# Self attention of a decoder layer: units per head, masks added in the pass for the maximum, outputs turned by the product, weights of q and k streamed

## What is computed

```python
h = x * rsqrt(mean(x * x) + EPS) * norm_w
q, k, v = (proj(w) for w in (w_q, w_k, w_v))        # 16 heads of 64
ll = einsum('bhnqd,bhnkd->bhnqk', qw, kw) * scale   # windows of 512: one per batch
ll = where(causal, ll, NEG)
scores = (einsum('bsd,do->bso', h, scorer_w) + scorer_b)[..., 0]
_, idx = top_k(scores, 128)                         # 128 tokens of the 512, by score
lg = where(idx <= pos, einsum('bhsd,bhgd->bhsg', q, kg) * scale, NEG)
attn = softmax(concatenate([ll, lg]))               # chosen tokens stand twice
o = attn[local] @ v + attn[chosen] @ vg
return x + o @ w_out
```

## Time and profile before

| what | value |
| --- | --- |
| median of 3 runs | 2310.07 us (2309.79 to 2315.15) |
| profiled execution | 2321.41 us, its span 2319.7 us |
| TensorE busy | 2134.8 us, 92% |
| VectorE busy | 1345.7 us, 58% |
| ScalarE busy | 844.9 us, 36% |
| GpSimd busy | 431.3 us, 19% |
| self attention | about 0 to 1556 us, eight batches, 184 us each |
| cross attention | about 1560 to 2080 us |
| routed block | the rest |

### The profile page before, as it was taken

The page is one execution under the profiler, slowest core; times in us unless marked ns, Lnnn a source line. Parts: engine busy times, 40 slices in busy tenths (PEclk is TensorE's granted clock), DMA queues, the critical chain, the costliest instruction groups (busy, mean ns, idle before and its releaser), DMA issues. The chain is left out here.

```text
span 2319.7 us, 35694 instructions
## 1 busy us (share of the span) xinstructions
PE 2134.8 (92%) x12029; PEld 1665.7 (72%) x12029; DVE 1345.7 (58%) x3145; ACT 844.9 (36%) x1541; POOL 431.3 (19%) x669
## 2 busy tenths in 40 slices
PE   3999999999999999999999999978898989978899
PEld 2886787688588688678768858846787888854543
DVE  5584376278177258437627817735787878745500
ACT  2442343244144144234324414415444444313210
POOL 2100100010010010010001001015676667520000
PEclk9999999999999999999999999998787878769899
DMA  5001000100100100100010010012013112150000
GB/s 190 1 2 33 24 1 16 41 1 5 52 1 1 56 1 1 33 24 1 15 42 1 3 54 1 1 56 62 26 59 130 57 57 66 51 199 1 1 0 18
DMA packets 46136, 80.23 MB, mean 35 GB/s; under 512 B 10067, under 2 KB 10067, under 8 KB 45448
## 3 DMA queue, kind: packets, MB, share of 16 engines
q1 hardware_dynamic: 45320, 75.85, 9.8%
q0 software_dynamic: 640, 2.10, 0.2%
HBM read 60.11 MB, written 17.83 MB: 34 GB/s over the span
## 5 line engine op out<-in xcount | busy, mean ns | idle before, releaser
L403 ACT ACTIVATE probs<-s_bank,nmax 128x512 f32<-128x512 f32 (+3 forms) x512 | 249.4, 525 | 369.1 <-DVE nmax L534 266.8
L686 PE MATMUL o_bank<-vals,probs_t 128*128 128x65 f32 x2560 | 329.1, 272 | 0.1
L686 PEld LDWEIGHTS o_bank<-vals,probs_t 128*128 128x128 f32 x2560 | 312.5, 192 | 13.3 <-DVE probs_t L542 13.0
L534 DVE TENSOR_REDUCE nmax<-s_bank 128x1 f32<-128x512 f32 (+2 forms) x384 | 184.5, 509 | 189.0 <-PE s_bank L663 185.4
L710 PE MATMUL pj_bank<-w_o,o_t 128*128 128x512 f32 x512 | 221.8, 594 | 6.0 <-ACT o_t L411 6.0
L542 DVE COPY probs_t<-pt_bank 128x512 f32<-128x512 f32 x320 | 218.1, 682 | 2.2 <-PE pt_bank L671 2.0
L671 PE MATMUL pt_bank<-ident,probs 128*128 128x128 f32 x1280 | 194.9, 275 | 15.7 <-DVE o_t L449 15.7
L659 PE MATMUL s_bank<-k_twice,q_both 128*128 128x512 f32 (+3 forms) x512 | 190.1, 373 | 2.1 <-DVE k_lo L522 2.1
L317 POOL TENSOR_TENSOR idle<-ones 128x4 f32<-128x4 f32 x41 | 8.2, 200 | 978.2 <-DMA probs<-in_x 976.1
L710 PEld LDWEIGHTS pj_bank<-w_o,o_t 128*128 128x128 f32 x512 | 96.6, 190 | 126.5 <-issue 126.5
L518 DVE SCALAR_TENSOR_TENSOR q_both<-pj_bank,q_both 64x512 fp32r<-64x512 f32 x128 | 88.2, 689 | 141.8 <-ACT q_both L390 139.2
(11 more groups left out here) (268 smaller groups left out, 4223.0 us busy)
## 6 DMA issues: line engine op xcount, KB each, us to landing
xb<-in_x SPq DMA_DIRECT2D x9, 1024.0 KB, 5.6
xt<-x SPq DMA_DIRECT2D x36, 256.0 KB, 2.8
probs<-in_x SPq DMA_DIRECT2D x32, 256.0 KB, 2.6
x<-probs SPq DMA_DIRECT2D x32, 256.0 KB, 2.0
am<-in_L_ffn_attention_mask SPq DMA_DIRECT2D x8, 1024.0 KB, 5.3
out<-x SPq DMA_DIRECT2D x32, 256.0 KB, 2.1
w_sb<-in_L_ffn_w SPq DMA_DIRECT2D x2, 4096.0 KB, 20.4
o_t<-in_L_attn_w_v SPq DMA_DIRECT2D x2, 1024.0 KB, 9.9
```

The costliest lines, as they stand in the source:

```text
L403: ins = nc.scalar.activation(probs[:, i % 2, c0:c0 + nk], s_bank[i % 2][:, c0:c0 + nk], ACT.Exp, bias=nmax[:, i % 4, n:n + 1])
L534: ins = nc.vector.tensor_reduce(nmax[:, i % 4, n:n + 1], s_bank[i % 2][:, c0:c0 + nk], AX.X, ALU.max, negate=True)
L686: ins = nc.tensor.matmul(o_bank[slot][:, o0:o0 + VW], probs_t[:, i % 2, c0 + P * kt:c0 + P * kt + P], vals[:, kt, 2 * p + h, :], start=(kt ...
```

## The change

What it does:

- A head has three units (`UNITS = 3`, `unit_rows`): 512 columns; 128 and 384; 256 columns. A pair of heads has six steps. The product with the values is made once a head, at every third step.
- The causal matmul is gone. `masks` holds what is subtracted from the scores: -ln 2 for chosen keys, and 1e30 for later ones. It is built once a batch: `tw` on TensorE, `build_masks` on VectorE. q is projected with a minus sign. VectorE's pass over the scores now adds the mask, writes the sum to `probs` (a ring of four) and takes the minimum, which is the negated maximum; each such pass is followed by a read of the accumulator.
- ScalarE's exponential works in place in `probs` and writes its row sums, `den`. VectorE takes their reciprocal (`r`), GpSimd multiplies the rows by it.
- After the turn ScalarE writes the high part `p_hi` and VectorE the low part `p_lo`. `vals` holds high and low parts of the values side by side; it is the stationary operand of 16 matmuls per pair in fp32r, with `p_hi` and then `p_lo` moving. The result stands turned, its two halves are added by a ScalarE copy and a VectorE sum into `o_t`. The `ot` entries are gone.
- `q_lo` and `k_lo` are no entries of their own: VectorE makes q's low part in the entry `q`. For k, ScalarE copies the product to `k_raw` and the other head's rows to `k_twice`; GpSimd makes the own rows and the low part `k_low`, four instructions.
- High and low parts of w_q and w_k are written to DRAM by pairs at the start (`store_parts`) and loaded pair by pair, 1 MB each, into `w_qk` (two slots).
- In the cross attention the shift by the maximum moves from GpSimd into ScalarE's exponential, one instruction per head, eight in place of one. Sums of products there and in the routed block use `scalar_tensor_tensor` with an accumulated output.

```diff
-UNITS = 5
-NU = NPAIR * UNITS
+NH = 2 * NPAIR
+UNITS = 3
+NU = NH * UNITS
+RING = 4
...
-    for g in range(NU + 7):
-        p, u = divmod(g, UNITS)
+    for g in range(NU + 4):
+        if 1 <= g < NU + 1:
+            plan.append(("r", g - 1))
         if g < NU:
             plan.append(("s", g))
         if 2 <= g < NU + 2:
             plan.append(("t", g - 2))
-        if 3 <= g < NU + 3:
-            plan.append(("pv", g - 3))
-        if g < NU and p + 1 < NPAIR and u < 4:
-            plan.append((("q", "q_lo", "k", "k_lo")[u], p + 1))
+        if g >= 6 and g % UNITS == 0:
+            plan.append(("pv", g // UNITS - 2))
+        p, u = divmod(g, 2 * UNITS)
+        if p + 1 < NPAIR and u in (1, 4):
+            plan.append(("q" if u == 1 else "k", p + 1))
...
+                    if kind == "r":
+                        pl.wait_ge(den_ready, b * NU + i + 1)
+                        for n, (_, c0, nk) in enumerate(unit_rows(i % UNITS)):
+                            part = probs[:, i % RING, c0:c0 + nk]
+                            ins = nc.gpsimd.tensor_tensor(part, part, rden[:, i % 4, n:n + 1].broadcast_to((P, nk)),
+                                                          ALU.mult)
+                        ins.then_inc(norm_ready, 1)
...
+                    if kind == "s":
+                        act.wait_ge(max_ready, b * NU + i + 1)
+                        for n, (_, c0, nk) in enumerate(unit_rows(i % UNITS)):
+                            part = probs[:, i % RING, c0:c0 + nk]
+                            ins = nc.scalar.activation(part, part, ACT.Exp, bias=nmax[:, i % 4, n:n + 1], scale=-1.0,
+                                                       accum_out=den[:, i % 4, n:n + 1])
+                        ins.then_inc(p_ready, 1)
+                    if kind == "t":
...
+                        act.wait_ge(pt_ready, ready)
...
+                        nc.scalar.copy(p_hi[:, h % 2, TURNED_AT[u], :],
+                                       pt_bank[slot][:, 0:P * n].rearrange("p (n k) -> p n k", k=P)).then_inc(hi_ready, 1)
...
+                        if h % 2 == 0 and u == 0:
+                            pe.wait_ge(q_lo_ready, b * NPAIR + p + 1)
+                            pe.wait_ge(k_other_ready, b * NPAIR + p + 1)
+                            pe.wait_ge(k_low_ready, b * (2 * NPAIR) + 2 * p + 2)
                         if i >= 2:
-                            pe.wait_ge(p_ready, b * NU + i - 1)
+                            pe.wait_ge(max_ready, b * NU + i - 1)
...
+                        parts = [(p, k) for p in (p_hi, p_lo) for k in (0, 3, 1, 2)]
+                        for n, (part, k) in enumerate(parts):
+                            ins = nc.tensor.matmul(o_bank[i % 2][:, 0:P * (TT - k)], vals[:, k, i, :],
+                                                   part[:, i % 2, KEYS_AT[k], :], start=(n == 0),
+                                                   stop=(n == len(parts) - 1))
```

More of the change, by code:

```diff
@@ L365, in _ @@
                 act.wait_ge(w_loaded[i % 2], 16 * (i // 2 + 1))
-                nc.scalar.copy(w_hi[n][:, :, 512 * hw:512 * hw + 512],
-                               o_t[:, DC * (i % 2):DC * (i % 2) + DC, :]).then_inc(split_hi, 1)
+                if n == "v":
+                    nc.scalar.copy(wv_hi[:, :, 512 * hw:512 * hw + 512], staged(i)).then_inc(split_hi, 1)
+                else:
+                    if i >= 4:
+                        act.wait_ge(w_stored[i % 2], 32)
+                    view, parts = by_pair(i)
+                    for r in range(NPAIR // 2):
+                        ins = nc.scalar.copy(parts[0][:, r], view[:, r])
+                    ins.then_inc(split_hi, 1)
                 if i == 1:
@@ L385, in _ @@
+                    if kind == "q":
                         slot, ready = pj(b, (kind, i))
                         act.wait_ge(pj_ready, ready)
+                        if i == 0:
+                            act.wait_ge(w_stored[0], 64)
+                        for h in range(2):
+                            own = head_rows(h)
+                            ins = nc.scalar.activation(q_both[own, i % 2, h, :], pj_bank[slot][own, :], ACT.Copy,
+                                                       scale=-HD ** -0.5)
+                        ins.then_inc(q_hi_ready, 1)
@@ L464, in rank, with build_masks, scores_in @@
                     step(nc.vector.tensor_tensor(cnt[:, 0, :], cnt[:, 0, :], cnt[:, 1, :], ALU.add))
-                    if b is not None:
-                        dv.wait_ge(v_ready, n * (2 * TT))
-                    nc.vector.tensor_scalar(twice[:, :], cnt[:, 0, :], TOPK - 0.5, 1.0, ALU.is_lt,
-                                            ALU.add).then_inc(twice_ready, 1)
+                    nc.vector.tensor_scalar(chosen[:, :], cnt[:, 0, :], TOPK - 0.5, -LN2, ALU.is_lt,
+                                            ALU.mult).then_inc(chosen_ready, 1)
+            def build_masks(b):
+                slot, ready = pt(b, ("tw", 0))
+                dv.wait_ge(pt_ready, ready)
+                row = pt_bank[slot]
+                for at, n in ((0, 3), (640, 2), (1024, 1)):
+                    done.mark(nc.vector.tensor_copy(masks[:, at:at + P * n], row[:, 0:P * n]))
+                for at, k in ((384, 3), (512, 0), (896, 2), (1152, 1)):
+                    ins = nc.vector.tensor_tensor(masks[:, at:at + P], row[:, P * k:P * k + P], later_keys[:, :], ALU.add)
+                done.wait(dv)
+                ins.then_inc(masks_ready, 1)
+            def scores_in(b, i):
+                dv.wait_ge(s_ready, b * NU + i + 1)
+                if i < 2:
+                    dv.wait_ge(x1_out[i], b * (16 * TT // 2) + 1)
+                elif i >= RING:
+                    dv.wait_ge(pt_ready, pt(b, ("t", i - RING))[1])
             def normed(b, n, c):
@@ L689, in _ @@
[L689 to L698 removed]
+                            pe.wait_ge(o_ready, b * NH + i - 1)
```

437 lines of the change are left out of this document (236 added, 201 removed).

## The result

The changed kernel took 3019.49 us (median of 4 runs, 3013.13 to 3022.46), the kernel before 2310.28 beside it: 1.306 times as long, 95% interval 1.303 to 1.308. Forecast were 3050 (2800 to 3260).

A forecast was written before the change was run, and what follows sets the result against it. A serial ring of VectorE and ScalarE plus GpSimd's stall was to make a pair 23.1 us; 2310 + 580 (self attention) + 160 (clock) + 5 (startup) - 5 (cross attention) = 3050 us, range 2800 to 3260.

The forecast's parts named there:

- 73 and the clock's 20: Self attention, per batch: 8 pairs at 6.4 us more, plus 13, 4 and 4.5 us, is 73; the clock's 160 us came on top.
- near 60%: Self attention: TensorE's busy share forecast for the profile after; above 90% at full clock would prove the prediction wrong.
- The ring: Self attention: VectorE and ScalarE wait for each other in turn, 20.4 us a pair against 16.7 before; main case, chance 0.62.
- faster: Rival: VectorE and ScalarE get round faster than 14 us a pair, TensorE's saving counts, 2130 us; chance 0.05.
- The stall for k: Next pair's first scores wait for GpSimd's k rows and low part: 5.8 us, 2.7 a pair beyond the ring, 56 times.
- TensorE's share: Self attention: TensorE's work falls 2.8 us a pair, from 16.7 to about 14.
- The row sum: ScalarE's exponentials also write row sums: 0.1 us each, between nothing and 0.17; 0.4 us a head.
- The clock: Self attention: TensorE's waits lower its granted clock, costing 2.5 us a pair, 160 us in all (0 to 320).
- The start: Startup: 8 MB are written and two loads wait for stores, 5 us (0 to 15).
- Cross attention: Shift moved from GpSimd to ScalarE's eight exponentials: -5 us, between -25 and 20.
- Weights streamed: 1 MB per pair, asked for nine units early on SP: costs nothing.
- the prediction's slow rate: GpSimd's k rows at the 1.678 us of its broadcast instruction: 1.7 us more a pair, some 110 us, left out.

The follow-up runs named there:

- the searched order: Changed kernel's instructions, plus tiny ones ahead of maxima, placed by a search that stepped the engines' orders (turn and low part at g-4): 2263.96 us, 0.978 of the kernel before.
- k first: Changed kernel with the projections of q and k exchanged, k behind a pair's second unit and q behind the fifth: 3042.72 us.
- fillers: Changed kernel with 16 more 512-column matmuls on TensorE ahead of a pair's first scores, overwritten by these: 2989.61 us.
- low parts late: Changed kernel with VectorE's two low parts (turned unit's and q's) one unit later in its order: 2940.13 us.
- turn late: Changed kernel with the turn of a unit at g-3 instead of g-2, its product with the values too: 2937.7 us.
- everything late: Changed kernel with low parts late, k and q projected earlier, GpSimd's k instructions spread, reciprocal behind the next maximum, turn still at g-2: 2947.73 us.

## Why the prediction was right, and where it was not

The time, the sign and the size by stage came out: 88 us a batch for 93 forecast (73 and the clock's 20), the shortest pair 26.3 us for a plain pair of 25.6, TensorE's wait for k 56 times. TensorE was busy 71% of a batch (197 of 277 us) where "near 60%" was forecast. That the order makes the 31%, and not the work, the searched order shows. Point by point:

- **The ring.** Its instructions are as priced (maximum of 512 columns 0.68, low part 0.69, high part 0.56 to 0.59). VectorE waits 589 us for ScalarE and ScalarE 822 for VectorE. But the step from "the ring takes 20.4 us" to "the ring is the bound" left out that other chains run through the same engines and hold the pair when the ring is open (that they are nearly as long is inferred from the gains of 79, 82 and 137; no run measures a chain alone). Opening it brought 79 us, where that reading made me expect 470. The rival "faster", in which TensorE's share counts as soon as the ring is open, was wrongly tied to this one ring.
- **The way back to TensorE** was missing. The prediction listed who waits within VectorE and ScalarE, but not how long a unit needs from scores to turn against the two units of lead. Before, the turn needed the exponential alone; now reciprocal and GpSimd's scaling stand between, and a unit is a sixth of a pair instead of a fifth. In the two units shown above it took 10.0 and 7.1 us.
- **The stall for k** was measured at 5.4 us on TensorE and 3.4 on VectorE, priced as 2.7 on the path. That it is a term to be added was not borne out: with k first it went from TensorE's waits, others came in its place, and the time rose by 23 us. Spreading k and q gained only with the other two opened (376 us between 2882.84 and 2506.93, a head's output and the reciprocal placed later with them).
- **TensorE's share**: 2.8 us a pair less forecast. In the searched order a batch has 166.3 us of TensorE at a clock of 0.98, 182.3 before: 2.0 a pair. The gain that came is 6.8 us a batch, where 8 x 2.0 would be 16.
- **The row sum** was taken at 0.1 us each, between nothing and 0.17. It is an instruction of its own:

```profile
L484 ACT ACTIVATION_READ_ACCUMULATOR probs<-probs,nmax 128x1 f32 x512 | 95.7, 187 | 0.0
L484 ACT ACTIVATE probs<-probs,nmax 128x512 f32<-128x512 f32 x128 | 92.4, 722 | 383.4 <-DVE nmax L651 383.4
```

  Its 187 ns overlap with the exponential and the copy; in spacing it costs 0.09 to 0.10 us, as forecast. The exponential itself, now from SBUF, takes 0.72 us for the 0.69 of the earlier trace rows.
- **The clock**: 160 us forecast. A batch stands at 0.80; fillers at one of its waits returned 30. How much the others cost was not measured apart.
- **The start**: 5 us forecast (0 to 15), 13 found. **Cross attention**: -5 forecast, -13 found, in range. **Weights streamed**: no wait for them shows among the waits above, as forecast.

That the number was this good is partly luck: the chains left out added little to the one that was priced, the stall of 2.7 us stands in the sum though no run shows it as a term of its own, and of the clock's 160 us the runs show 30.

## What to carry to other kernels

In a kernel whose engines follow written orders, list every loop of waits that a unit goes round (here VectorE with ScalarE, a unit's way back to the matmul engine against its lead, the operands of the next pair), and not the first that exceeds the old bound: here opening one of three brought 3%, and moving the work behind TensorE's largest wait brought nothing. Price an edit by stepping all the orders with measured durations: that found the order with the last 243 us (175 expected), which no single wait had shown, though it missed on the row sums (75 for 6). Take the price of an instruction from the spacing of starts, not from its duration. And separate the work of a change from its order: this one cost 31% as ordered and gained 2% with the same instructions placed later (and a tiny one added per unit). Of these 49 us the cross attention gives 13.

## What the runs showed of the hardware

**Small savings did not add up.** The row sums left out brought 6 us, with the fillers 43. Orders that differ (low parts late; turn late; everything late) have the same batch to 0.1 us:

```profile
1121.52:1387.76 266.24, 191.00 (x794) 144.24 (x793) 106.72 (x317) 101.49 (x244) 93.15 (x122) 0.83 0.13 44
...
1126.56:1392.80 266.24, 189.77 (x794) 147.62 (x793) 108.18 (x317) 100.60 (x244) 93.14 (x122) 0.85 0.13 44
...
1124.06:1390.30 266.24, 192.87 (x794) 145.79 (x793) 107.31 (x364) 100.85 (x244) 93.80 (x122) 0.83 0.13 44
```

From the second batch to the sixth each of the three repeats this length to 0.1 us. The changed kernel has 276.5 on average with and without row sums. In the searched order the same batches differ, from 179.2 to 183.7 us. So a difference of some us a batch between two kernels of this kind is no clean price of an edit, the 79, 82 and 72 above among them. What holds these batches together was not shown; that the changes of the clock do it fits the fillers, but no run tests it.

**A shared port, seen.** In the searched order VectorE's products for the token scores, both operands in SBUF, fell beside GpSimd's rows of k:

```profile
1033.55 0.99 DVE L535 SCALAR_TENSOR_TENSOR o_t<-xb,sw 128x512 f32<-128x512 f32 x1
1034.13 2.75 POOL L410 TENSOR_TENSOR k_twice<-k_raw,ones 64x512 fp32r<-64x512 f32 x2
1034.58 1.40 DVE L535 SCALAR_TENSOR_TENSOR o_t<-xb,sw 128x512 f32<-128x512 f32 x1
...
1036.96 3.29 POOL L418 TENSOR_TENSOR k_low<-k_raw,k_twice 64x512 fp32r<-64x512 f32 x2
...
1049.28 2.15 POOL L410 TENSOR_TENSOR k_twice<-k_raw,ones 64x512 fp32r<-64x512 f32 x2 [0.19 <-ACT k_raw L477]
...
1051.51 2.65 POOL L418 TENSOR_TENSOR k_low<-k_raw,k_twice 64x512 fp32r<-64x512 f32 x2
```

Alone (724.67 to 727.5 us in the changed kernel's trace) the product takes 0.67 to 0.69 us and GpSimd's two rows 2.15 and 2.65; together up to 1.40 in the lines above, 2.75 and 3.29. The Trainium skill, SBUF — State Buffer, "SBUF: two separate sides", names this pair of operand forms as one that locks the port. The trace agrees as far as both engines were held up; who waited for whom it does not show. In the changed kernel the rows of k took 2.15 and 2.60 beside the ring's instructions, which read PSUM, so the 110 us of the prediction's slow rate rightly stayed out.
